# A new step order on four engines, and a bank table in place of bank rotation, in an adaLN block

## The reference, cut to what matters

```python
h = _layernorm(x) * (1 + ca) + sa
x = x + ga * attn_ref(h, guidance)       # differences, 64 guides, softmax, windowed sum over 8 steps
h = _layernorm(x) * (1 + cb) + sb
x = x + gb * ffn_ref(h, ...)             # two layers of the following
# layer: q, k, v = shift(x) @ wqkv; l2norm and scale of q, k; rotary
#        attention of 8 heads in windows of 64 with the window before; x = x + o @ wo
#        h = layernorm(shift(x)) * g + b; a, g = split(h @ w1 + b1); x = x + (a * gelu(g)) @ w2 + b2
```

## Time and profile before

| | us |
|---|---|
| median of 3 runs | 955.89 |
| lowest and highest run | 953.37, 961.61 |
| span of the profiled execution | 957.5 |
| PE busy in it | 778.8 (81%) |
| DVE, ACT, POOL busy | 665.8, 660.0, 544.8 |

### The profile page before, as it was taken

How to read it: one execution, slowest core, us unless ns; L and a number is a source line. 1 busy time by engine, 2 the same in 40 slices (tenths; PEclk the granted TensorE clock), 3 DMA queues, 4 the chain that set the end, 5 groups by cost and what they waited for, 6 DMA issues and landing times.

```text
span 957.5 us, 19956 instructions
## 1 busy us (share of the span) xinstructions
PE 778.8 (81%) x7439; PEld 566.8 (59%) x7439; DVE 665.8 (70%) x1575; ACT 660.0 (69%) x1545; POOL 544.8 (57%) x326
## 2 busy tenths in 40 slices
PE   5977888778788888878879779878978888878884
PEld 5855656555565755555566665556666566556652
DVE  4667775868777866676786877576677766686732
ACT  2355758777776857868775866877676877768682
POOL 3176741858675544585766643393967762675700
PEclk9888999999999999999989989999899999999997
DMA  7000000000000000000000000000000000000000
GB/s 214 1 11 13 1 2 1 2 1 2 1 1 24 2 1 12 13 1 1 1 2 1 23 1 12 12 1 1 2 1 1 12 2 12 2 1 1 1 1 22
DMA packets 12710, 10.02 MB, mean 10 GB/s; under 512 B 1088, under 2 KB 11720, under 8 KB 12616
## 3 DMA queue, kind: packets, MB, share of 16 engines
q1 hardware_dynamic: 12616, 8.77, 3.0%
HBM read 6.67 MB, written 2.10 MB: 9 GB/s over the span
## 4 chain that ended last, share of the span: by engine, by line
PE 34%; DVE 22%; ACT 18%; issue 12%; POOL 12%; DMA 0%; POOLq 0%; SPq 0%; ACTq 0%; DVEq 0%
ACT probs L1040 6%; PE pair L737 6%; POOL roots L1561 5%; PE dense L894 4%; DVE qk L1285 3%; POOL qk L1609 3%; DVE space L1486 3%; PE mixed L783 3%; PE dense L975 2%; DVE neg_max L1307 2%; DVE q_norm L1491 2%; PE dense L858 2%; PE mixed L848 2%; PE dense L859 2%; PE dense L860 2%
## 5 line engine op out<-in xcount | busy, mean ns | idle before, releaser
L1609 POOL TENSOR_TENSOR qk<-space 128x512 f32<-128x512 f32 x128 | 178.8, 1402 | 26.1 <-DVE q_norm L1491 23.0
L1561 POOL TENSOR_TENSOR roots<-powers,minus_half 128x32 f32<-128x32 f32 (+1 forms) x33 | 174.8, 5296 | 17.0 <-DVE powers L1499 16.1
L1040 ACT ACTIVATE probs<-pair,neg_max 128x128 f32<-128x128 f32 x512 | 139.1, 397 | 11.3 <-DVE neg_max L1307 10.7
L975 PE MATMUL dense<-wq_hi,h_hi 128*128 128x512 f32 x192 | 93.6, 488 | 50.1 <-DVE space L1486 24.1
L1606 POOL TENSOR_TENSOR space<-space,tables 128x512 f32<-128x512 f32 x64 | 86.9, 1358 | 58.4 <-ACT space L1167 58.4
L1486 DVE TENSOR_TENSOR space<-dense,tables 128x512 f32<-128x512 f32 x128 | 87.5, 683 | 44.0 <-ACT space L1167 43.7
L1307 DVE TENSOR_REDUCE neg_max<-pair 128x4 f32<-128x512 f32 x128 | 81.3, 682 | 31.5 <-PE pair L822 31.4
L1163 ACT ACTIVATE squares<-dense 128x512 f32<-128x512 f32 x128 | 79.0, 618 | 32.6 <-PE dense L977 32.1
L737 PE MATMUL pair<-eye_s,probs 128*128 128x128 f32 x512 | 77.8, 285 | 24.5 <-ACT probs L1040 24.4
L1491 DVE TENSOR_REDUCE q_norm<-squares 128x8 f32<-128x512 f32 x128 | 86.4, 675 | 0.0
L975 PEld LDWEIGHTS dense<-wq_hi,h_hi 128*128 128x128 f32 x192 | 38.2, 199 | 78.8 <-issue 65.6
(11 more groups left out here) (210 smaller groups left out, 1880.7 us busy)
## 6 DMA issues: line engine op xcount, KB each, us to landing
x_in<-n_L_attn_embeddings_dram SPq DMA_DIRECT2D x8, 256.0 KB, 3.0
out_dram<-hn SPq DMA_DIRECT2D x8, 256.0 KB, 2.3
qk<-in_L_ffn_wqkv_dram SPq DMA_DIRECT2D x1, 1536.0 KB, 8.7
qk<-in_L_ffn_w_dram SPq DMA_DIRECT2D x1, 682.0 KB, 10.3
wo_s<-in_L_ffn_wo_dram SPq DMA_DIRECT2D x2, 256.0 KB
o_t<-in_L_wmod_dram SPq DMA_DIRECT2D x1, 384.0 KB, 4.2
band_s<-const_band_dram SPq DMA_DIRECT2D x1, 256.0 KB, 5.4
probs<-const_rotary_dram SPq DMA_DIRECT2D x1, 256.0 KB, 9.8
```

The source lines that it names most:

```text
L975: pe.matmul(to[:, :], h_hi[:, rows], wq_hi[:, layer, cols], start=True, stop=False)
L1040: last = act.activation(probs[:, ring, hh, :], banks[m][:, hh * P:(hh + 1) * P], ACT.Exp, bias=neg_max[:, ring, hh:hh + 1], scale=1.0)
L1561: return pool.tensor_tensor(to, of, minus_half[0:of.shape[0], 0:of.shape[-1]], ALU.pow)
L1609: pool.tensor_tensor(qk[s][:, t, m * INNER:(m + 1) * INNER], turned_c[:, t % 2, m, :], turned_s[:, t % 2, m, :], ALU.add).then_inc(added, 1)
```

## The change

The order of the steps in all four lists is new. The lists hold the same steps as before: 685 on PE, 595 on ACT, 555 on DVE and 243 on POOL. They are written as one list for each engine, each step with its turn and slot in front. No instruction of a step's own code changes. On PE a step stands on average 2.1 places from where it was, and at most 17. The bank of each use comes from a string of digits, `BANK_OF_USE`, one digit for each of the 400 uses of a dense bank; the count of former uses of the same bank, which the waits need, is kept for each bank.

```diff
@@ -39,334 +39,327 @@
-        turn = {">": 1, "<": -1}.get(word[0], 0)
-        slot, name = word.strip("<>").split(":")
-        found.append((turn, int(slot), tuple(int(part) if part.isdigit() else part for part in name.split("."))))
+        place, name = word.split(":")
+        turn, slot = place.split("/")
+        found.append((int(turn), int(slot), tuple(int(part) if part.isdigit() else part for part in name.split("."))))
...
-        3:setup.silu 3:setup.mod 3:new.turn 3:setup.guide 3:setup.gate 3:new.dots 3:setup.warm.0
...
+        -1/3:setup.silu -1/3:setup.mod -1/3:new.turn -1/3:setup.guide -1/3:new.dots -1/3:setup.warm.0
+        -1/3:setup.gate -1/3:new.mix -1/3:new.sum -1/3:setup.rows -1/3:setup.warm.1 -1/3:setup.warm.2
...
+BANK_OF_USE = (
+    "0120120120102120001201020210212021020120102102120120120120102102112012002102102102121020210201201021202"
...
@@ -400,14 +393,15 @@
-    def __init__(self, turns):
+    def __init__(self):
         self.place = {}
-        place = 0
-        for i in range(-1, turns + 1):
-            for turn, slot, step in ORDER["pe"][i + 1]:
-                for n in range(BANKS_OF.get(step[:2], 0) if step[0] != "a" else 0):
-                    self.place[(i + turn, slot, step, n)] = (place % DENSE_BANKS, place // DENSE_BANKS)
-                    place += 1
+        held = [0] * DENSE_BANKS
+        banks = iter(BANK_OF_USE)
+        for i, slot, step in ORDER["pe"]:
+            for n in range(BANKS_OF.get(step[:2], 0) if step[0] != "a" else 0):
+                b = int(next(banks))
+                self.place[(i, slot, step, n)] = (b, held[b])
+                held[b] += 1
@@ -629,9 +623,8 @@
-            for i in range(-1, turns + 1):
-                for turn, slot, step in ORDER[name][i + 1]:
-                    take(i + turn, slot, step)
+            for i, slot, step in ORDER[name]:
+                take(i, slot, step)
```

More of the change, by code:

```diff
@@ L372 @@
+BANK_OF_USE = (
+    "0120120120102120001201020210212021020120102102120120120102102112012002102102102121020210201201021202"
+    "0120120120120121021021020121022102102102102102012012012012020102120121021021021021020121021201210021"
+    "1021201201212012012012102011200012120120120120210210210210210121021020120120121020120120012012020122"
+    "0101210210210212012010210210202102102102012012012012010210201210210210210121201020120120120120120120")
 BANKS_OF = {(FF, "stats"): 1, (FF, "norm"): 1, (FF, "up"): 2, (FF, "down"): 1, (STORE, "turn"): 1,
@@ L427, in adaln_block @@
     turns = units // 2
-    bank_turns = BankTurns(turns)
+    bank_turns = BankTurns()
     with ExitStack() as ctx:
```

623 lines of the change are left out of this document (304 added, 319 removed).

## The result

The changed kernel takes **882.54 us** (median of 4, 881.19 to 886.59), the kernel before 955.47 on the same chip. The ratio is 0.923, 95% interval 0.918 to 0.927. Forecast were 920 us, in a range of 892 to 950: the direction was right, the size was not, and the time lies under the range. Less than half of the gain had been seen.

A forecast was written before the change was run, and what follows sets the result against it. No engine was taken as saturated: PE idles in many short waits for close dependencies or banks. Nine terms summed to 46.3 us; a fifth given back left 37, so 957.5 - 37 = 920 us, range 892 to 950.

The forecast's parts named there:

- term 7: PE's waits for `space` and `v`: fewer tiles whose bank is soon wanted again, net 3.8 us off.
- Mix to out: Attention, DVE normalises in between: fewer outs close behind their mix, 6.6 us off PE's waits for `o_rows`.
- Score to flip: Attention, DVE's maxima and ACT's exponentials in between: a fifth of PE's waits for `probs` goes, 5 us.
- Feed-forward and shift: Waits for `hn`, `shifted`, `h_lo`: half goes outside the last unit, 10.7 us; the last unit keeps its 4.16 and 3.09.
- Banks of new.dots: DVE frees them only after the guides' softmax; the table sends tiles to the third bank instead, 8.5 us off.
- Function tables: ACT's table loads: two of 1.28 us in the last turn go, 36 of 38 left, 2.6 us off.
- The head: Set-up: moved gate copies and ACT's second `setup.hi` lose between nothing and 2 us, taken as 1.
- A fifth given back: Whole kernel: of the 46.3 us removed, a fifth returns as steps meet the next wait, so 37 us stay.
- PE's busy time stays near 779, and less if the clock holds.: Sign to look for in the profile: PE busy about 779 us, less if its clock holds.
- More comes: Rival, chance 0.15: all 46.3 us stay and PE's clock gains at most 16 us more, giving 895 us.
- Given back: Rival, chance 0.20: DVE's and ACT's own queues take back three quarters of the gain, 946 us, range 941 to 953.
- DVE and POOL collide: Rival, chance 0.07: DVE's unit-length steps and POOL's sums block each other, 972 us; sign: a median up half a microsecond.

The follow-up runs named there:

- old_spaced: Kernel before, banks in rotation, with 25 exchanges of neighbours on PE alone, so no score, mix or out stands directly behind its producer: 987.06 us, ratio 1.029.
- old_dots: Kernel before, same order, banks in rotation except 14 uses in the 9 us behind each new.dots, moved to the third bank: 990.11 us, ratio 1.029.
- new_tight: Changed kernel with 26 pairs of steps that were neighbours in the kernel before made neighbours again, on PE alone: 922.42 us, ratio 0.963 to the kernel before.
- new_nowarm: Changed kernel without its warm-up transposes, whose results nobody reads: 886.55 us, ratio 0.922 to the kernel before.
- old_joint: Kernel before with 86 neighbour exchanges on PE, banks in rotation; ACT, DVE and POOL turned to the new order as far as possible: 1362.94 us, ratio 1.424.

## Why the prediction was wrong

**Which direction, and which body.** Right: most of the loss was in the body, spread over many short stops, and PE's order and banks could take it back. The chance of 0.81 for faster stood on that.

**Which steps failed.** Two. The sum put PE's own time at nothing and gave no reason, and it fell by 26.2 us. And term 7, the other bank waits, was mis-sized: 3.8 us forecast, 19.2 measured.

**The steps of the sum**, forecast and measured as the fall of the named waits of PE:

1. *Mix to out*, 6.6: `o_rows` 15.4 to 7.4, 8.0.
2. *Flip to mix*, 5.5: `probs_t` 9.5 to 5.5, 4.0.
3. *Turn to score*, 4.6: `k_t` 13.3 to 7.1, 6.2.
4. *Score to flip*, 5.0: `probs` 24.4 to 17.9, 6.5.
5. *Feed-forward and shift*, 10.7: `hn`, `shifted` and the two `h_lo` 28.7 to 16.2, 12.5; the last unit's 4.16 stayed, its 3.09 became 2.74.
6. *Banks of new.dots*, 8.5: 10.5 to 2.7, 7.8.
7. *Other bank waits*, 3.8: `space` and `v` 38.4 to 19.2, **19.2**. This is the term that was mis-sized, by 15.4 us.
8. *Function tables*: 36 loads are left of 38, as forecast. But one of the two that went stood at L1090, and one is left in the last turn at L1033, where the prediction had none.
9. *The head*, a loss of 1: instead 0/3 ends 10.8 us earlier, though its first projection starts 2.3 us later and PE meets a new wait of 9.7 us.

Terms 1 to 6 came to 45.0 us where 40.9 were forecast, so counting how many steps stand between two was a fair measure of a family's own wait, as it was in old_spaced (17.3 us). It says nothing of the kernel's time: old_spaced was slower. Term 7 was counted in the same way, by how soon a bank is wanted again in PE's list. But a bank comes free when DVE or ACT gets to it in its list, as old_dots shows. The table sends 397 of 400 uses to the bank that these lists free first, and with rotation in the same order it is 330, at 34.8 us more of waits for banks and 47 us in all.

**"A fifth given back"** held as a share. The named waits fall by 64.2 us, PE's idle time by 51.9: 12.3 us, 19%, came back. The largest new waits are the 9.7 for `step_t` and 5.6 more for `qk`.

**"PE's busy time stays near 779, and less if the clock holds."** The second half happened, and the forecast had left it to a rival with a ceiling of 16 us; the sum of 46.3 has no term for it. It was 26.2 us of own time, and it has two parts. One is the clock: PE had 62.1 us of own time at 1.2 GHz and has 21.8. What that costs can be read in the last unit of the changed kernel, where the clock rises in the midst of a row of matmuls that all move 128x512. Two stretches, then the timeline:

```profile
865.00:868.00 3.00, 3.00 (x8) 2.34 (x7) 0.52 (x1) 0.69 (x1) 0.00 (x0) 0.50 0.00 0
869.00:870.00 1.00, 1.00 (x6) 0.68 (x5) 0.50 (x1) 0.38 (x1) 0.00 (x0) 1.00 0.00 0
```

```profile
867.17 0.63 PE L851 MATMUL dense<-h_hi,w_hi 128*128 128x512 f32 x1
867.60 0.63 PE L852 MATMUL dense<-h_lo,w_hi 128*128 128x512 f32 x1
...
869.23 0.40 PE L851 MATMUL dense<-h_hi,w_hi 128*85 128x512 f32 x1
869.46 0.39 PE L852 MATMUL dense<-h_lo,w_hi 128*85 128x512 f32 x1
```

At 1.2 GHz they start 0.43 us apart, at 2.4 GHz 0.23. Of a microsecond of own time at the low level nearly half is lost. The other part is the stop itself: a step behind a stop has a longer own time (in the trace of before at full clock, on average, an `a.out` 0.66 us against 0.50, a projection tile 0.94 against 0.75). The lines above show one reason: at full clock a matmul lasts 0.39 us and the next starts after 0.23, so without a stop the first matmul of a step overlaps the one ahead, and behind a stop its whole length counts. The ends of matmuls are modelled in the profile, so this part may as well be put down to the stops. A straight line through the twelve rows of the table gives own = 719 + 0.22 x stops + 0.48 x own at 1.2 GHz, within 3 us for all but new_tight (6 us). It was fitted on these rows and is no more than a summary of them. By it the clock is 40.3 x 0.48 = 19.5 us and the 39 stops fewer are 8.6, together 28 where 26.2 were measured. The ceiling of 16 held for what it was worked out from: in the body own time at 1.2 GHz goes from 34.4 to 9.8 us, 11.8 us by the line. It left out the head (19.7 to 6.2), the end (8.0 to 5.8) and the part of the stops. How much of the head's share cost anything is open: in new_nowarm 17 us more of it, with the transposes gone, cost at most some 5.

So 46.3 - 9.3 = 37 became 64.2 - 12.3 + 26.2 = 78.1 us: 26.2 of own time, and 19.5 more of waits gone than the 44.7 that terms 1 to 7 had, 15.4 of it in term 7.

**The rivals.** *More comes* was the nearest, and its 895 still too timid; its premise that nothing comes back did not hold. *Given back*, with three quarters, is out. *DVE and POOL collide*: the mechanism is there and its price is small. DVE's unit-length step has a median of 2481 ns against 2292, 84.8 us in all against 78.7. The bound named, half a microsecond on the median, wasn't reached, POOL's median moved by 2 ns, and the kernel got faster. The Trainium skill's rule ("SBUF — State Buffer", section "Who interferes with whom") agrees with the trace in kind: 17 of the 32 take over 2.4 us where 9 did, for 6 us of DVE. It didn't decide anything. A larger part of DVE's 19 us is a short instruction, `powers`, with 20.0 us in all against 11.7. Before and after:

```profile
L1499 DVE TENSOR_SCALAR powers<-q_norm x32: 170/181/1264, 58.7 to 891.7; 128x32 f32<-128x32 f32 x32
```

```profile
L1492 DVE TENSOR_SCALAR powers<-q_norm x32: 168/628/1243, 65.5 to 818.0; 128x32 f32<-128x32 f32 x32
```

There 12 of 32 last over 0.3 us before and 19 after, and every one of these starts while an instruction of POOL runs and ends 0.04 us after that instruction.

**What I had not asked.** The forecast treated the change as a sum of separable repairs of PE's list. The four edits of the old order, to PE's list or the banks alone, made it 2.9 to 4.4% slower, though each was aimed at a wait of the profile. Two of them put many uses in a row on one bank, so they don't show that no table can help the old order. The new order loses 40 us by 26 small moves on PE. In other parts the change can be had: the four new orders with rotation keep 26 of the 73 us, and the new order from turn 1 on keeps nearly all (0.925). With the lists of different orders paired, 42% are lost. Not tried was the whole new PE list with the old lists of the other engines, or the reverse, which by my reading of the lists would lock up. So what each engine's new list gives by itself stays open.

## What to carry to other kernels

In a schedule with one strict list for each engine, a wait in the profile tells what a family of stops costs, but each repair that I made in one list alone moved it to the next pair and lost: change the lists together, banks included. Read when a shared bank comes free from the list of the engine that empties it, not from how long that takes. And when PE is the bound, count removed stops twice: the idle time, and PE's own time behind them and at the lower clock, here another half (26 on 52 us).

## What the runs showed of the hardware

- The low clock can cost far less than its length: in new_nowarm 34 us more of it in the head, 17 of them own time of PE, came with at most some 5 us more in all, with 160 transposes less to do.
- The same 7439 matmuls kept PE busy for 753 us in the changed kernel and for 920 in old_joint, with 22 us of own time at 1.2 GHz in the one and 376 in the other. "Busy time of PE" is no constant of the program.
- A short DVE instruction (`powers`, 0.18 us) that starts while POOL works can last to 0.04 us behind the end of POOL's instruction, up to 1.26 us: 12 of 32 times before, 19 of 32 after.
- DVE got slower by 19 us in busy time in the changed kernel while the kernel got faster by 73: here the rise of an engine's busy time showed as no loss.
